# A block kernel on one core: the low-rank rows move to another tile, and the wait for the sent q/k parts moves with them

## What is computed

```python
h = layernorm(x) * (1 + ca) + sa
x = x + ga * attention(h)          # 16 heads, phi(q), phi(k) with 128 features, cumulative sums
h = layernorm(x) * (1 + cb) + sb
# experts: w = weights of the 2 best of 4 by softmax(h @ Wg.T + bg)
base     = h @ Wi.T                                  # 1024 wide
lora_low = einsum('bsd,erd->bser', h, A)             # 4 experts x rank 4
lora     = einsum('bser,efr->bsef', lora_low, B)
hid      = relu(base[:, :, None, :] + lora)
out      = einsum('bse,bsed->bsd', w, einsum('bsef,df->bsed', hid, Wo))
x = x + gb * out
```

## Time and profile before

| | us |
|---|---|
| median of 3 runs | 839.67 |
| lowest, highest | 836.02, 840.61 |
| profiled execution, its own time | 835.22 |
| its span in the trace | 833.4 |
| TensorE busy, share of the span | 765.5, 92% |
| VectorE busy | 546.9, 66% |
| ScalarE busy | 410.9, 49% |
| mean granted clock of TensorE | 0.984 |

### The profile page before, as it was taken

How to read it: one execution, slowest core, us unless ns; L and a number is a source line. 1 busy time by engine, 2 the same in 40 slices (tenths; PEclk the granted TensorE clock), 3 DMA queues, 4 the chain that set the end, 5 groups by cost and what they waited for, 6 DMA issues and landing times.

```text
span 833.4 us, 16957 instructions
## 1 busy us (share of the span) xinstructions
PE 765.5 (92%) x6138; PEld 603.4 (72%) x6138; DVE 546.9 (66%) x1289; ACT 410.9 (49%) x758; POOL 47.0 (6%) x62
## 2 busy tenths in 40 slices
PE   2989998999899999999999998999999998999596
PEld 2767767876698766977678765987678776887366
DVE  5546666776667775776666766677656766665456
ACT  2365545564456444654455544564446543555122
POOL 1101000010001000010000100010000100010000
PEclk9979999999999999999999999999999999999989
DMA  8680072203702064111722037020731017110000
GB/s 271 149 196 2 24 207 57 76 0 94 189 0 75 0 194 89 43 32 42 195 45 75 0 103 180 0 75 0 202 81 57 18 50 200 33 52 1 1 1 26
DMA packets 46540, 65.37 MB, mean 78 GB/s; under 512 B 8716, under 2 KB 22840, under 8 KB 46392
## 3 DMA queue, kind: packets, MB, share of 16 engines
q1 hardware_dynamic: 46520, 65.10, 29.0%
HBM read 39.87 MB, written 25.17 MB: 78 GB/s over the span
## 4 chain that ended last, share of the span: by engine, by line
PE 73%; DVE 14%; DMA 7%; issue 3%; ACT 2%; SPq 1%; DVEq 0%; POOL 0%; ACTq 0%
PE pa L513 11%; PE prod L528 7%; DMA qk_parts<-qk_l 6%; PE ring L492 6%; PE pa L379 5%; PE pa L381 4%; PE pa L380 4%; PE prod L547 4%; PE pa L619 4%; PE ring L379 4%; PE ring L497 3%; PE ring L380 3%; PE ring L381 3%; PE prod L513 2%; PE ring L695 2%
## 5 line engine op out<-in xcount | busy, mean ns | idle before, releaser
L513 PE MATMUL pa<-phq,phkT 128*128 128x128 f32 x896 | 115.1, 276 | 0.0
L513 PEld LDWEIGHTS pa<-phq,phkT 128*128 128x128 f32 x896 | 107.8, 191 | 2.3 <-issue 1.6
L820 ACT ACTIVATE phq<-ring 128x512 f32<-128x512 f32 x96 | 58.9, 614 | 90.6 <-PE ring L492 89.7
L1077 DVE TENSOR_TENSOR am_phk<-pa,const 128x512 f32<-128x512 f32 x112 | 74.2, 685 | 32.0 <-PE pa L513 32.0
L1230 DVE SCALAR_TENSOR_TENSOR am_phk<-ring,am_phk 128x512 f32<-128x512 f32 x64 | 44.2, 691 | 55.4 <-PE ring L695 55.4
L379 PE MATMUL pa<-wo_r,qk_r 128*128 128x256 f32 x256 | 72.1, 282 | 0.6 <-DVE qk_l L1235 0.6
L381 PE MATMUL pa<-wo_l,qk_r 128*128 128x256 f32 x256 | 72.1, 282 | 0.0
L380 PE MATMUL pa<-wo_r,qk_l 128*128 128x256 f32 x256 | 71.8, 281 | 0.0
L882 ACT ACTIVATE qk_r<-phq 128x512 fp32r<-128x512 f32 x64 | 40.5, 632 | 63.3 <-DVE phq L1239 62.8
L528 PE MATMUL prod<-am_phk,v_ones 128*32 128x256 f32 x1024 | 61.9, 382 | 4.6 <-DVE tg L1108 4.6
L379 PE MATMUL ring<-h_r,wi_r 128*128 128x512 f32 x128 | 57.7, 451 | 3.6 <-DVE am_phk L1230 2.9
(11 more groups left out here) (189 smaller groups left out, 1566.2 us busy)
## 6 DMA issues: line engine op xcount, KB each, us to landing
xq<-qk_parts SPq DMA_DIRECT2D x48, 512.0 KB
qk_parts<-qk_r SPq DMA_DIRECT2D x32, 256.0 KB, 3.3
qk_parts<-qk_l SPq DMA_DIRECT2D x32, 256.0 KB, 3.6
tok<-in_L_attn_x SPq DMA_DIRECT2D x8, 512.0 KB, 4.6
xr<-in_L_attn_x SPq DMA_DIRECT2D x8, 512.0 KB, 3.7
out_x<-tg SPq DMA_DIRECT2D x16, 256.0 KB, 2.2
norm_parts<-norm_r SPq DMA_DIRECT2D x16, 128.0 KB, 3.5
norm_parts<-norm_l SPq DMA_DIRECT2D x16, 128.0 KB, 5.1
```

The costliest lines, as they stand in the source:

```text
L513: mm = pe.matmul(score_bank(q, a)[:, tt], phkT[:, q % 2, a, tt], phq[:, q // 2 % 2, 2 * (q % 2) + a, tt], start=True, stop=True)
L820: act.activation(dst, src, ACT.Exp).then_inc(exp_done.sem, 1)
L1077: dve.tensor_tensor(am[:, 2 * (q % 2) + a, :].rearrange("p (c t) -> p c t", c=NT), score_bank(q, a)[:].rearrange("p (c t) -> p c t", c=NT) ...
```

## The change

`low` becomes the view `am_phk[0:96, 2, 0]`. The tile is float32, so the writes to it are cast to F32R and the reads no longer cast back. ScalarE no longer waits for `qk_out` ahead of L861; it waits for them ahead of the first write of `g_r` in the loop over f (k = 0), behind its wait for `g_sum`. Number, shape and order of all computing instructions and DMAs stay.

```diff
-        g_r, g_l, low = qk_r[:, 0:3], qk_l[:, 0:3], qk_r[0:LROWS, 3]
+        g_r, g_l = qk_r[:, 0:3], qk_l[:, 0:3]
         r2, lg = am[:, 0:2], am[:, 2]
+        low = am_phk[0:LROWS, 2, 0]
...
                 act.activation(lg, ring[2][:], ACT.Copy).then_inc(lg_done.sem, 1)
-                if front_next:
-                    for signal in qk_out:
-                        wait(act, signal, n + 1, signal.per)
-                act.activation(low, ring[2][0:LROWS, :], ACT.Copy).then_inc(low_high.sem, 1)
+                act.activation(low.bitcast(F32R), ring[2][0:LROWS, :], ACT.Copy).then_inc(low_high.sem, 1)
...
                         wait(act, g_sum, n, k + 1)
+                        if k == 0 and front_next:
+                            for signal in qk_out:
+                                wait(act, signal, n + 1, signal.per)
                         if k >= 3:
                             wait(act, wo_mm, n, k - 2)
                         act.activation(g_r[:, k % 3, :], g[:, k % 4, :], ACT.Copy).then_inc(g_high.sem, 1)
...
-                    dve.tensor_tensor(dst, low.bitcast(F32), src[0:LROWS],
+                    dve.tensor_tensor(dst, low, src[0:LROWS],
                                       ALU.mult).then_inc(low_masked.sem, 1)
...
-                dve.tensor_tensor(low[64:96, :], lg[64:96], low[64:96, :].bitcast(F32),
-                                  ALU.subtract).then_inc(low_split.sem, 1)
+                dve.tensor_tensor(low[64:96, :].bitcast(F32R), lg[64:96], low[64:96, :], ALU.subtract).then_inc(low_split.sem, 1)
```

## The result

The changed kernel took 827.21 us (median of 4 runs, 822.88 to 827.81), the kernel before 840.14 on the same chip; the ratio is 0.9846, 95% interval 0.9815 to 0.9878. On a second chip it took 824.35 against 839.43, 0.9832 (0.9804 to 0.9860). The forecast was 824.0 in a range of 819.5 to 830. The profiled execution took 827.64, span 825.9; it had been forecast at 822.0. Two runs over 1.5% above the fastest of their kernel, 1245.69 of the kernel before on the second chip and 852.02 of the kernel before with its gap filled, are left out of the ratios.

What follows compares the result with a forecast made beforehand. The prediction took the chain through the qk_parts transfer, not TensorE alone, as the bound. Less 10.8 us (blocks) and 2.4 (clock), the profiled 835.22 became 822.0; between 822 and 826.5 it took 824.0, range 819.5 to 830.

Steps and rivals of the forecast that it cites:

- Steps 1 to 3: ScalarE's rounding copy to `low` starts 2.48 us earlier, VectorE's L1257 follows, and the router starts 2.39 us earlier.
- Step 4: Mask transposes on TensorE: base products take 0.9 us of the router's lead, leaving 1.50 us a block, 10.3 in all.
- Step 5: Masks to first expert product: 0 to 0.15 us more a block, 0.5 us taken in all.
- Step 6: ScalarE's wait moves ahead of the first rounded write of g (L882): costs nothing, 2 us without cover.
- Steps 7 and 8: Using the am_phk tile for `low` costs 0, bound 1 us each way; SP's queue is not touched.
- The order of landings: Transfers SP issues: norm parts, issued last, can't be reported before the qk parts (315.05, 315.7).
- The clock: TensorE's granted clock in the loop: two falls of about 1.2 us expected to vanish, 2.4 us more.
- If their excess is more falls of the clock at this gap: The earlier runs' median, 4.45 us above the profiled execution: if from clock falls ahead of the masks, it goes too.
- The first: Clock not won back, or falls at another gap instead: 828.9 us; 10%.
- The wait moved: Wait only moves to VectorE's L1222, or the copy wasn't what held the router: no gain, 839.7 us; 5%.
- The slower case: Wait at ScalarE's L882 becomes the long one, stalling g copies and TensorE's output products: 847 us; 2%.
- the half gain: VectorE's path is longer than counted, so masks or L1222 come 0.8 us late: 834.2 us; 3%.

Runs made afterwards that it cites:

- the later router: Changed kernel with small chained VectorE instructions that nobody reads ahead of the router: 822.64 us with three, 831.96 with eight, 836.22 with eleven.

## Why the prediction was right, and where it was not

- *Steps 1 to 3.* L859 0.49 behind L858, forecast 0.50. L1258 0.69 behind L859, forecast 0.70. The router was forecast 0.45 behind the start of the logit transposes and is at 0.44. The masks are no longer late for TensorE.
- *Step 4, 1.50 us a block, 10.3 in all.* Measured without falls: 94.9 against 96.3 to 96.5, so 1.4 to 1.6, 1.5 in the middle. The loss of 0.9 us of the router's lead to TensorE's base products is what kept the forecast from 2.4 us a block, and the later router measured it at 0.81.
- *Step 5.* Masks to first expert product is 1.56 us, not 1.45 to 1.53: 0.04 won a block, 0.3 in all instead of 0.5. The last block's row was no full guide to the loop.
- *Step 6.* The waits' price can now be read. L883, 321.72, starts 0.17 us after the end of L1240 for k = 0, and 0.04 after it for k = 1; before, L882 started 0.04 after L1239. So two satisfied waits with their registers cost ScalarE 0.13 us, and nobody waits for it (0.13 is less than the 0.6 us of cover that the prediction counted). The transfer had landed at 313.46 at the latest, 8.3 us ahead of L883, where the prediction counted 9:

```profile
321.72 0.63 ACT L883 ACTIVATE qk_r<-phq 128x512 fp32r<-128x512 f32 x1 [0.24 <-DVE phq L1240]
...
324.73 0.63 ACT L883 ACTIVATE qk_r<-phq 128x512 fp32r<-128x512 f32 x1 [0.61 <-DVE phq L1240]
...
320.86 0.69 DVE L1240 TENSOR_TENSOR phq<-phq,am_phk 128x512 f32<-128x512 f32 x1
324.01 0.68 DVE L1240 TENSOR_TENSOR phq<-phq,am_phk 128x512 f32<-128x512 f32 x1
```

- *Steps 7 and 8.* The tile costs nothing (1.0018, interval across 1); SP's queue goes on as before.
- *The order of landings.* The prediction argued that the norm parts, issued last, can't be reported before the qk parts. That doesn't hold for both of them: in the kernel before norm_r, issued at 308.94, landed 4.2 us later, so at 313.1, and qk_l, issued at 307.43, only at 315.05. The part that counts for the change, norm_l, was the last (315.7). Nothing in the sum rested on it.
- *The clock.* The loop's part, 2.4 us in the profiled execution, came as said: no fall in the six intervals of either profile of the changed kernel. The step that failed is the one behind it, "If their excess is more falls of the clock at this gap". How much of the excess of 4.45 us is that isn't shown, as the kernel before has one profile. But start and last block have falls of their own, of varying length, and I had only a subordinate clause for the last block's. The profiled execution of before had a short last interval (93.7), that of the changed kernel a long one (97.4): comparing the two makes the gain 3.8 us too small, and the change didn't make that difference, since the same last block took 93.5 behind the loop with one extra store. With some 1.4 in the start this is nearly all of the 5.6 by which 827.64 missed 822.0.
- *The median.* 824.0 was a compromise between "near 822" (the excess goes) and 826.5 (it stays). On the first chip the medians differ by 12.9 us, which is the 13.2 of the worked-out terms alone, and 827.21 lies at the second branch; on the second chip they differ by 15.1, as if 1.9 of the excess had gone with it. So the terms were right, and that 824.0 itself is met within 0.4 us on the second chip and missed by 3.2 on the first says nothing for the compromise; the hit is luck.
- *The rivals.* The first (828.9, the clock not won back) has the right size for some runs and the wrong place: what falls is outside the loop. The wait moved to L1222's successor only under three extra stores. The slower case and the half gain didn't come. (The half gain's sum is off by 0.3: 0.8 us late in seven blocks leaves 10.8 - 5.6 = 5.2, so 834.5 and not 834.2.)

## What to carry to other kernels

A rounding copy that reuses a tile still being sent pulls every instruction behind it on two queues into the transfer's wait; ask which of them need the copy at all, then take the gain from the idle time of the engine that bounds (9.1 us here), not from the wait itself (16.3). Follow the freed engine until something else is late: here TensorE's own products, which take up 0.9 us of the lead, and the next transfer with 3.5 us in hand. Before a forecast of the median, split the profile into setup, loop and last block and look at the granted clock of each: a change that closes gaps in the loop did nothing here for the falls in the other two.

## What the runs showed of the hardware

The same instructions in the last block took 93.5 us from masks to masks in one execution (the changed kernel with one extra store) and 97.4 in two others (the changed kernel's two profiles), as the granted clock was at 0.5, the 1.2 GHz level, once or twice in them; with the gaps filled by matmuls that nobody reads it took 91.42 at a clock of 1.00. I had not expected work without use to be worth 2 to 6 us. The Trainium skill, "TensorE: Matmul & The Clock Gate", section "Part 1: The HAM clock gate (the "warmup" mystery)", says that activity is what releases the slow state and that the point of the change varies from run to run; these traces agree: no 0.5 in that interval once the gaps were filled, and 6.8 or 17.1 us of it for the same instructions without. A store of 768 KB ahead of four of 256 KB delayed the last landing by 1.9 us, not by the 3.8 that I had estimated from its bytes at some 200 GB/s (the kernel before moves 191 GB/s from 300 to 307 us and 233 from 307.4 to 315.05).
